# A landing wait on POOL after every eight indirect transfers in a four-layer graph network

## The reference, cut to what matters

```python
edge_index = stack([src, dst])
x = layernorm(x + L0(x))   # z = x; y = z W0; 3 times: z = segment_sum(w_e * z[dst], src); y += z Wk
x = layernorm(x + L1(x))   # typed attention over (src -> dst): q[dst] . k[type, src], softmax by dst, sum of v
x = layernorm(x + L2(x))   # leaky_relu(x_l[src] + x_r[dst]) . att, softmax by dst, sum of x_l[src]
x = layernorm(x + L3(x))   # q[src] . k[dst], softmax by src, values summed by dst
```

## Time and profile before

| | us |
|---|---|
| median of three runs, without the profiler | 9746.5 |
| span of the profiled execution | 13177.8 |
| POOL busy in it | 7027.7 (53%) |
| PE busy | 6872.9 (52%) |
| DVE busy | 6549.5 (50%) |
| ACT busy | 2082.2 (16%) |

### The profile page before, as it was taken

One profiled execution on the slowest core, in us unless ns is written; L12 is line 12 of the kernel. 1 busy time (PEld: TensorE's weight loads), 2 busy tenths in 40 slices (PEclk: granted clock), 3 DMA queues, 4 the chain that ended last, 5 costly groups with the idle time before them and its releaser, 6 DMA issues. The chain is left out here.

```text
span 13177.8 us, 169349 instructions
## 1 busy us (share of the span) xinstructions
PE 6872.9 (52%) x37679; PEld 6012.4 (46%) x37680; DVE 6549.5 (50%) x22663; ACT 2082.2 (16%) x6208; POOL 7027.7 (53%) x7417
## 2 busy tenths in 40 slices
PE   5555444445554555100384555656666566665555
PEld 4444333335554555100234455456665465654444
DVE  6444455555555555200265555755556344455555
ACT  4222100001110111000121111311222111122222
POOL 6555566646664666777205555245553555535554
PEclk6555555556666666555687777877787555556766
DMA  0000011111111111010143222111112211112232
GB/s 19 1 1 1 21 44 44 44 42 42 42 43 40 42 42 43 16 22 8 50 157 79 74 74 74 56 38 39 39 39 65 52 38 38 38 47 77 79 81 74
DMA packets 436083, 614.60 MB, mean 47 GB/s; under 512 B 176625, under 2 KB 312133, under 8 KB 435173
## 3 DMA queue, kind: packets, MB, share of 16 engines
q0 software_dynamic: 257024, 486.93, 14.5%
q1 hardware_dynamic: 178369, 119.49, 3.2%
q10 hardware_dynamic: 292, 3.41, 0.1%
HBM read 520.17 MB, written 89.19 MB: 46 GB/s over the span
## 5 line engine op out<-in xcount | busy, mean ns | idle before, releaser
L1094 POOL DMA_INDIRECT hop_rows<-hops,k_src_gather x1568 | 1479.3, 943 | 1077.3 <-issue 435.9
L1137 PE MATMUL hop_sums<-hop_rows,hop_weighted 128*128 x4992 | 1159.9, 405 | 1110.7 <-DVE k_x L1184 736.1
L1137 PEld LDWEIGHTS hop_sums<-hop_rows,hop_weighted 128*128 128x128 f32 x4992 | 1009.7, 300 | 1201.7 <-issue 1200.4
L1443 POOL DMA_INDIRECT l_pass_rows<-related,k_dst_typed x832 | 786.2, 945 | 1216.8 <-POOLq L74 517.6
L1443 POOL DMA_INDIRECT l_pass_rows<-left_table,k_dst_other x832 | 786.6, 945 | 895.7 <-DVE l_pass_terms L1815 490.5
L1938 POOL DMA_INDIRECT l_weigh_rows<-row_table,l_weigh_ring x832 | 813.0, 977 | 733.8 <-ACT l_weigh_ring L1902 466.3
L1443 POOL DMA_INDIRECT l_pass_rows<-key_table,k_src_gather x784 | 739.5, 943 | 766.6 <-DVE l_pass_scores L1752 387.3
L726 POOL DMA_INDIRECT src_sorted<-src_scatter_records,src_scatter_places x784 | 750.6, 957 | 606.3 <-DVE src_scatter_places L714 393.6
L1538 PE MATMUL l_pass_sums<-l_pass_zero 128*128 128x272 bf16 (+1 forms) x1210 | 262.7, 306 | 1454.0 <-DVE l_total L1632 1005.2
L1094 POOL DMA_INDIRECT hop_rows<-in_x,k_src_gather x784 | 739.6, 943 | 456.4 <-issue 220.8
L1292 POOL DMA_INDIRECT dst_sorted<-rec,dst_places x784 | 809.2, 1032 | 262.1 <-issue 262.1
(11 more groups left out here) (467 smaller groups left out, 18342.8 us busy)
## 6 DMA issues: line engine op xcount, KB each, us to landing
related<-l_tables_rows SPq DMA_DIRECT2D x50, 1024.0 KB, 4.4
hop_rows<-hops,k_src_gather POOLq DMA_INDIRECT x1568
l_pass_rows<-related,k_dst_typed POOLq DMA_INDIRECT x832
l_pass_rows<-left_table,k_dst_other POOLq DMA_INDIRECT x832
l_weigh_rows<-row_table,l_weigh_ring POOLq DMA_INDIRECT x832
src_sorted<-src_scatter_records,src_scatter_places POOLq DMA_INDIRECT x784
hop_rows<-in_x,k_src_gather POOLq DMA_INDIRECT x784
dst_sorted<-rec,dst_places POOLq DMA_INDIRECT x784
```

Source lines behind the costliest of these rows:

```text
L1094: nc.gpsimd.indirect_dma_start(rows[:, s * G + g, :], None, table_in, bass.IndirectOffsetOnAxis(ap=o.gather[:, c:c + 1], axis=0),).then_in ...
L1137: last = nc.tensor.matmul(sums[:, b, g, :], weighted[:, s % SLOTS, g, :], rows[:, bass.ds(slots[g], 1), :], start=True, stop=True)
L1443: nc.gpsimd.indirect_dma_start(rows[:, s, g, :], None, table, bass.IndirectOffsetOnAxis(ap=index[:, c:c + 1], axis=0),).then_inc(got[s], 16)
```

## The change

Three waits are added on POOL, and nothing else is touched. In the hops and in the score passes POOL waits, after every second group of four, until that group has landed; in the scatter by destination after each eighth transfer, until that and the others on the last of the four semaphores have landed. The transfers before it in the eight are on other semaphores, which are not waited for.

```diff
@@ hop, POOL
                                                  bass.IndirectOffsetOnAxis(ap=o.gather[:, c:c + 1], axis=0),
                                                  ).then_inc(got[s], 16)
+                if n % 2 == 1:
+
+                    pool.wait_ge(got[s], (n // RING + 1) * 16 * G)
@@ scatter_ranked, POOL
             nc.gpsimd.indirect_dma_start(table, bass.IndirectOffsetOnAxis(ap=places[:, c:c + 1], axis=0),
                                          rec[:, c, :], None).then_inc(sent[c % SLOTS], 16)
+            if c % (2 * SLOTS) == 2 * SLOTS - 1:
+
+                pool.wait_ge(sent[SLOTS - 1], 16 * (c // SLOTS + 1))
@@ softmax_pass, POOL
                                                  bass.IndirectOffsetOnAxis(ap=index[:, c:c + 1], axis=0),
                                                  ).then_inc(got[s], 16)
+                if n % 2 == 1:
+
+                    pool.wait_ge(got[s], (n // ring + 1) * 16 * G)
```

## The result

The changed kernel takes **11240.0 us** (median of 3 runs, 11239.3 to 11247.1) where the kernel before takes 9746.5: 1.153 times the time, 95% interval 1.151 to 1.155. The forecast was 11080; the time lies 160 us above it and inside both ranges.

What follows compares the result with a forecast made beforehand. Unprofiled, POOL's issue of indirect transfers at 1.24 us each was taken as the bound; 9746.5 plus 1170 us of gather waits and 162 of scatter waits gave 11080 us, own range 10850 to 11300, 8-in-10 range 10200 to 11300.

Steps and rivals of the forecast that it cites:

- a sum: Whole kernel unprofiled: POOL's transfers 9008 us plus stretches without transfers 803 us make 9811, against 9746.5 measured.
- Rival 1: Hops, passes and scatter: consumers hide part, 0.6 us of each wait is free; 10650 us, with more slack 10200; chance 0.15.
- rival 3: Hops and passes: POOL stands behind each eighth transfer unprofiled too, so the waits change nothing; 9746 us; chance 0.05.
- the stretches without transfers: Start, before and between hops, after the scatter, between passes, end: times when POOL has no transfer, 803 us in all.
- POOL's own time: All stages: 5632 gathers at 1.248 us plus 1568 scatters at 1.262 us, 9008 us.
- the holding: In the profiled execution, PE's finished work reaches other engines late while POOL's transfers land; unprofiled runs have no room for it.
- The price of a wait: Hops, passes, scatter by destination: 1.95 us per gather group (600 waits, 1170 us), 1.65 per scatter group (98, 162 us).
- The pieces: Each added wait: landing 1.5 us (gather) or 1.2 (scatter), plus restart 0.76, less 0.30 that would pass anyway.
- the scatter's 162 us: Scatter by destination: 98 added waits at 1.65 us each.
- The estimate from the Trainium skill: Gather waits: a DMA fit of 2.15 us from issue for 64 KB gives 1.67 us a wait, 1160 us added in all, 10910.
- the scatter's waits count in full: Scatter by destination: 750 us of dense work beside it end before its 990 us, so all 162 us count.
- Rival 2: Passes and dense work under the scatter: holding is real in all runs, POOL's stops let signals through; 8970 us, half 9350; chance 0.11.

Runs made afterwards that it cites:

- the longest pause: Changed kernel with its 698 waits replaced by POOL scratch fills (twelve, then seven more), no transfer waited for: 10964.8 us, 1.127 of the kernel before (9728.8) in its session.

## Why the prediction was right, and where it wasn't

**What bounds the kernel: right.** That the unprofiled kernel is bound by POOL's issue was argued from a sum (9008 + 803 = 9811 against 9746.5). The runs show it: 10.0 to 10.1 us per eight in the stages without waits, POOL's 46 us for the consumers, and a pause that costs its own length. Rival 1 (consumers hide 0.6 us of each wait) is out by the same rows, and rival 3 (nothing) by the 1494 us. That the sum closed within 0.7% was partly luck, though. It took the stretches without transfers from the held profile, 803 us; in the profile after they are 654 (21 and 20 us between the hops, not 57 and 62; 44 before the weighing, not 118). POOL's own time was put at 9008 us and is 9069 in the trace of the longest pause, once its pauses are taken off. Two errors of opposite sign left 9811 beside 9746.5.

**Where the holding comes from: wrong.** The prediction took it for something of the profiled execution, and named a possible cause from the Trainium skill, "NOTIFIC — the notification-queue block", section 7.1. The profiles of the changed kernel and of the longest pause are free of it, and in four sessions the timed runs of the kernel before, 40 in all, have it. These 40, and the seven unheld runs of the kernel before beside the longest pause as well, each have a span and a granted clock on record (9727.0 us and 0.686 in one of the seven). So taking a profile doesn't make it by itself. The step that holds is the sum: 9746.5 leaves no room for holding. The step that fails is the one from there to "the profiler": the profile could as well be of another condition of the machine, and by all later runs it was. The records name the same chip number for the first held session and for the unheld one of the longest pause, so a chip's number doesn't tell the condition either. What does is open, and so is the mechanism of the holding.

**The price of a wait: the mis-sized term.** 1.95 us for a gather group and 1.65 for a scatter group were predicted. The six rows of the wait table give 1458.4 us over 583 gathers, 2.50, less 0.30: **2.20**; and 210.7 over 97 scatters, 2.17 less 0.30: **1.87**. 600 x 0.25 + 98 x 0.22 = 172 us, and the forecast was 160 short.

The pieces can be read one by one from the semaphore updates in the trace (medians). In hop 1 the last update comes 1.57 us behind the eighth gather's end, and the next transfer starts 0.82 us after it; 1.5 and 0.76 were predicted, so there the pieces were nearly right. In pass 1, whose rows have 1024 bytes instead of 512, the landing takes 1.79 us, and the idle is 2.85 on average. The rest is a few long idles (one of 12.0 us in pass 1, one of 11.2 in pass 3, one of 16.3 in the scatter), all near the start of a stage, where tables or lists are moved by other queues. The prediction took the landing of the third pass's very last group, when all else was quiet.

The scatter's mean hides two prices. While the tables of layer 1 are written beside it (4950 to 5340, 139 GB/s) and after that (10 GB/s), POOL's time line has:

```profile
5109.14 0.96 POOL L1295 DMA_INDIRECT dst_sorted<-rec,dst_places  x1 [2.86 <-DMA dst_sorted<-rec,dst_places]
...
5595.24 0.96 POOL L1295 DMA_INDIRECT dst_sorted<-rec,dst_places  x1 [1.43 <-DMA dst_sorted<-rec,dst_places]
```

In the quiet part a wait costs 1.43 - 0.30 = 1.13 us and not 1.65: the landing is 1.17 us, as predicted, but POOL starts again 0.27 us after it and not 0.76. So the scatter's 162 us came near the measured 98 x 1.87 = 183 because a restart taken too dear and a landing taken too quiet cancelled. That part was luck.

The estimate from the Trainium skill, "DMA: Bandwidth & Descriptors", section "Anatomy of one DMA — SWDGE (gpsimd) path", 1.67 us a gather wait, was too low by a quarter; the measurement decides.

**That the scatter's waits count in full: right.** The dense work ends before it; 27 us lie behind the scatter, 22 were assumed.

**Rival 2 (faster, because POOL's stop lets the signals through): right in the other condition.** It put 8970 against 9746.5, a ratio of 0.920; held, the change measures 0.925. Its terms: nothing from the hops (83 us measured), the dense work freed (352 us, 334 reckoned), the passes 306 x 2.4 = 730 us (565 measured, the period falls to 12.3 to 12.6 us, not 11.9). Its condition, "if the holding costs over 2 us per eight in an unprofiled run", was met in the held sessions and not in the unheld ones. Its chance of 0.11 was not a chance of the mechanism but of the condition in which the measurement would fall, and the profile couldn't tell that.

**What the profile after was to show.** POOL's idle of 2.2 to 2.7 us before each eighth: on average 2.17 to 2.85 by stage. Hops with 12.4 us per eight: 12.2 unheld, 12.4 held. Passes 12.3: yes in both. Scatter 1180 us: 1188. A span that falls to 12300: held it fell from 13166 to 12182, and in the profile shown above, unheld, to 11245.

## What to carry to other kernels

Before a change is costed from a trace, hold the trace's span against the times: here they differed by a third, they were of two conditions of the machine, and the change had a price in each. Where POOL's issue of indirect transfers is the bound, a wait for the landing of the last group costs its whole idle, here 2.2 us each on average, since it hides behind nothing. And compare kernels only with runs of the kernel before from the same session: here the verdict changed sign between sessions.

## What the runs showed of the hardware that was not expected

- The two conditions: the kernel before takes 9728 to 9750 us (10 runs of two sessions) or 13161 to 13383 us (40 runs of four sessions, with medians of 13185, 13188, 13191 and 13376), and never in between. POOL's gathers are the same in both: 0.944 to 0.947 us each (medians in the hops), 0.30 to the next.
- Held, what PE has finished reaches ACT, DVE and POOL up to several us late while POOL's transfers are issued and landing (0.35 us became 4.23 in the pair above). What holds it back is open. A pause of POOL of 0.98 or 1.33 us behind each eight transfers takes 1.8% or 4.2% off the time, the wait for the landing 7.5%.
- Unheld, the landing that POOL waits for depends on what else moves: in one and the same scatter the idle is 2.86 us beside 139 GB/s and 1.43 beside 10.
- Fills on POOL overlap: one of 128x832 takes 0.81 us, twelve of 128x69 together 1.17, less than the 0.17 to 0.18 at which each is listed would add up to (2.1).
